# Attention with the probabilities as the stationary operand: sums turned by DMA, projected in three fp16 passes, auxiliary units spread in six slots

## The reference, cut to what matters

```python
q = layernorm(x) @ w_q;  k = ctx @ w_k;  v = ctx @ w_v           # 16 heads of 64
attn = softmax(q k^T / 8)                                        # over 1444 context rows
x = x + tanh(g_xattn) * ((attn v) @ w_o + b_o)
X = layernorm(x)
X2 = X + self_attention(rmsnorm(X, norm1_w)) @ wo                # 16 heads of 8, over 100 tokens
h2 = rmsnorm(X2, norm2_w)
moe = shared(h2) + top-2 of 8 experts(h2)                        # each silu(h2 wg) * (h2 wu) @ wd
out = x + tanh(g_ffn) * (X2 + moe)
```

## Time and profile before

| | us |
|---|---|
| median of 3 runs (1532.3 to 1535.36) | 1532.89 |
| the profiled execution | 1536.03 |
| its span on the core, first to last instruction | 1534.3 |
| a batch in the middle | 79.2, or 81.2 with the loop's turn |
| TensorE, DVE, ScalarE, POOL busy in the span | 1374, 1060, 810, 580 |

### The profile page before, as it was taken

One profiled execution on the slowest core, in us unless ns is written; L12 is line 12 of the kernel. 1 busy time (PEld: TensorE's weight loads), 2 busy tenths in 40 slices (PEclk: granted clock), 3 DMA queues, 4 the chain that ended last, 5 costly groups with the idle time before them and its releaser, 6 DMA issues.

```text
span 1534.3 us, 28786 instructions
## 1 busy us (share of the span) xinstructions
PE 1374.3 (90%) x8776; PEld 839.2 (55%) x8776; DVE 1060.1 (69%) x1996; ACT 810.3 (53%) x1188; POOL 580.3 (38%) x702
## 2 busy tenths in 40 slices
PE   4769999999999999999999999899999999888898
PEld 4225555555555565555555555555555555456676
DVE  2777777767676767676767777677767676866665
ACT  1134646555555555555555565556565655554554
POOL 3023334333433434343334333434333433453454
PEclk7579999999999999999999999999999999899999
DMA  7020202020202010010202020202020100000000
GB/s 216 24 56 1 56 1 57 1 58 1 57 1 58 1 32 25 19 39 2 56 2 57 1 57 1 57 1 57 1 58 1 42 1 1 1 1 1 7 7 11
DMA packets 66966, 43.26 MB, mean 28 GB/s; under 512 B 52966, under 2 KB 62410, under 8 KB 66826
## 3 DMA queue, kind: packets, MB, share of 16 engines
q1 hardware_dynamic: 66826, 41.43, 10.7%
HBM read 15.38 MB, written 0.82 MB: 11 GB/s over the span
## 4 chain that ended last, share of the span: by engine, by line
PE 58%; DVE 18%; issue 12%; ACT 4%; POOL 3%; DMA 2%; DVEq 1%; SPq 0%; ACTq 0%; POOLq 0%
PE psum L756 15%; DVE mx L1240 7%; PE psum L816 7%; PE psum L737 6%; PE psum L741 6%; PE psum L739 6%; PE psum L769 4%; PE psum L856 3%; PE psum L808 3%; PE psum L782 3%; PE psum L843 3%; ACT p_hi L952 2%; DVE y_sb L1262 2%; POOL y_sum L575 2%; DVE mx L1274 1%
## 5 line engine op out<-in xcount | busy, mean ns | idle before, releaser
L951 ACT ACTIVATE p<-psum 128x800 f32<-128x800 f32 x384 | 321.1, 836 | 557.2 <-PE psum L741 555.2
L1240 DVE TENSOR_REDUCE mx<-psum 128x1 f32<-128x512 f32 (+1 forms) x624 | 387.6, 654 | 59.2 <-PE psum L816 55.3
L432 POOL TENSOR_TENSOR p_lo<-p,p_hi 128x800 f16<-128x800 f32 x128 | 244.0, 1906 | 482.3 <-ACT p_hi L952 469.3
L756 PE MATMUL psum<-p_hi,c_both 128*128 128x400 f16 x1536 | 390.3, 336 | 26.3 <-POOL p_lo L432 18.0
L952 ACT ACTIVATE p_hi<-psum 128x800 f16<-128x800 f32 x384 | 319.4, 832 | 0.0
L432 DVE TENSOR_TENSOR p_lo<-p,p_hi 128x800 f16<-128x800 f32 x256 | 258.8, 1011 | 54.6 <-issue 20.1
L816 PE MATMUL psum<-cT_both,qk_hi 96*128 96x512 f16 (+1 forms) x624 | 233.2, 388 | 67.3 <-DVE y_sb L1262 19.5
L756 PEld LDWEIGHTS psum<-p_hi,c_both 128*128 128x128 f16 x1536 | 146.7, 98 | 146.0 <-POOL p_lo L432 24.3
L737 PE MATMUL psum<-qk_hi,cT_both 97*128 97x400 f16 x768 | 195.2, 335 | 14.0 <-issue 9.5
L756 PE MATMUL psum<-p_lo,c_both 128*128 128x400 f16 x768 | 194.9, 335 | 0.0
L739 PE MATMUL psum<-qk_lo,cT_both 96*128 96x400 f16 x768 | 194.5, 334 | 0.0
(11 more groups left out here) (183 smaller groups left out, 1774.9 us busy)
## 6 DMA issues: line engine op xcount, KB each, us to landing
c_both<-c_new SPq DMA_DIRECT2D x16, 768.0 KB, 4.0
ctx_nat<-in_ctx_dram SPq DMA_DIRECT2D x16, 528.0 KB
wg<-in_L_ffn_e_gate_dram SPq DMA_DIRECT2D x1, 1024.0 KB, 5.3
wu<-in_L_ffn_e_up_dram SPq DMA_DIRECT2D x1, 1024.0 KB, 7.3
wd<-in_L_ffn_e_down_dram SPq DMA_DIRECT2D x8, 128.0 KB, 4.9
out_dram<-x SPq DMA_DIRECT2D x4, 200.0 KB
x<-in_x_dram SPq DMA_DIRECT2D x1, 600.0 KB
p<-in_L_xattn_w_q_dram SPq DMA_DIRECT2D x1, 512.0 KB, 3.8
```

What stands on the lines that cost most here:

```text
L432: engine.tensor_tensor(p_lo[0:m, i % 3, :, :], p32[0:m, i % 3, :, :], p_hi[0:m, i % 3, :, :], ALU.subtract).then_inc(lo_made(b, i)[0], 1)
L756: t = mm(outs[k], w[parity][0:m, j, :], p[0:m, i % 3, k, :], start=(j == 0 and w is c_hi and p is p_hi), stop=(j == CH - 1 and w is c_lo))
L951: a(p32[0:m, i % 3, :, :], src, ACT.Exp, scale=DH ** -0.5)
L1240: v.tensor_reduce(mx[:, rt, part:part + 1], bank[:, 0:w], AX.X, ALU.max)\
```

## The change

The product is turned round. Tiles of 128 (head, token) rows of the probabilities become the stationary operand and the context chunk, 97 columns wide (96 for its low part), moves. The 1600 rows make 6 tiles in the first half and 7 in the second (the last one padded), so the scores take 384 and 416 columns per matmul. The passes are p_hi c_hi, p_hi c_lo, p_lo c_hi, and p_lo is waited for only ahead of the third. The sums then lie with (head, token) on partitions. ScalarE copies them in two instructions, POOL's `normalise` multiplies them by the reciprocals and splits them in hi and lo, and SP turns both by DMA (`turn`) into aT. The projection is one auxiliary unit per half (7 and 9 heads), three fp16 passes per head summed in PSUM, and one DVE instruction adds it to x. add_heads, the reciprocals and the products with them are gone.

Auxiliary units are cut in sixths: after the first and second score pass, after the scores, after the first and second product pass, and at the end. y1 stands in unit 7, y0 in 20, ln in 8, and f one unit later up to unit 20. POOL makes the low part of nine units; norm_1 stands ahead of unit 9's, behind those of 5 and 7.

```diff
-    YB = [(0, 1, 2), (3, 4, 5), (6, 7)]
-    YW = D + 1
+    TILES, PER_BANK = (6, 7), (3, 4)
+    WIDE = (6 * P // 2, (ROWS - 6 * P) // 2)
+    ROW0 = (0, 6 * P)
+    PW = 2 * WIDE[1]
+    Y_HEADS = (range(0, 7), range(7, H))
+    Y_SCALE = 256.0
...
-    for n, i in enumerate((2, 3, 4)):
-        plan[i].append(("y1", n))
-    for n, i in enumerate((15, 16, 17)):
-        plan[i].append(("y0", n))
-    plan[6].append(("ln", 0))
-    plan[8].append(("xf", 0))
-    for n, i in enumerate((8, 9, 10, 11, 12, 13, 12, 13, 14, 15, 14, 15, 16, 17, 18, 19, 23)):
+    plan[7].append(("y1", 0))
+    plan[20].append(("y0", 0))
+    plan[8].append(("ln", 0))
+    plan[9].append(("xf", 0))
+    for n, i in enumerate((9, 10, 11, 12, 13, 14, 13, 14, 15, 16, 15, 16, 17, 18, 19, 20, 23)):
         plan[i].append(("f", n))
-    plan[20].append(("rs", 0))
+    plan[21].append(("rs", 0))
     plan[22].append(("h2", 0))
...
-    CTX_AT, Y0_AT = 0, 18
-    LO_POOL = (6, 8, 10, 12, 14, 16, 18, 20)
+    CTX_AT, NORM1_AT, ACC0_AT, NORM2_AT = 0, 8, 14, 22
+    LO_POOL = (5, 7, 9, 11, 13, 16, 18, 20, 22)
...
+    for n, unit in enumerate([("y1", 0), ("ln", 0), ("xf", 0)] + [("f", n) for n in range(16)] +
...
-        thirds = [[us[len(us) * k // 3:len(us) * (k + 1) // 3] for k in range(3)] for us in by_place]
-        return thirds, at
+        sixths = [[us[-(-len(us) * k // 6):-(-len(us) * (k + 1) // 6)] for k in range(6)] for us in by_place]
+        return sixths, at
...
         qk_hi = [sb(f"qk_hi{q}", [C + 1, RT * P], F16) for q in range(2)]
         qk_lo = [sb(f"qk_lo{q}", [C, ROWS], F16) for q in range(2)]
-        p32 = sb("p32", [P, 3, 2, GW])
-        p_hi = sb("p_hi", [P, 3, 2, GW], F16)
-        p_lo = sb("p_lo", [P, 3, 2, GW], F16)
-        acc_sb = [sb(f"acc_sb{g}", [C + 1, 2, GW]) for g in range(2)]
+        p32 = sb("p32", [P, 3, PW])
+        p_hi = sb("p_hi", [P, 3, TILES[1] * P], F16)
+        p_lo = sb("p_lo", [P, 3, TILES[1] * P], F16)
+        acc_sb = sb("acc_sb", [P, TILES[1], C + 1])
+        acc_rc = sb("acc_rc", [P, TILES[1]])
+        minus_one = sb("minus_one", [P, TILES[1]])
+        a_new = sb("a_new", [P, 2, TILES[1], P], F16)
+        aT = sb("aT", [P, 2, sum(TILES) * P], F16)
         mx = sb("mx", [P, RT, MP])
...
+            def turn(b, half):
+
+                t0, t1 = ROW0[half], ROW0[half] + TILES[half] * P
+                for k in range(2):
+                    wait_apart(sp, acc_norm, (b * 2 + half) * 2 + (k + 1))
+                    sp.dma_start_transpose(aT[:, k, t0:t1].rearrange("p (j k) -> p j k", k=P),
+                                           a_new[:, k, 0:TILES[half], :].rearrange("p j c -> p (j c)")).then_inc(at_in, 16)
...
                 for b, kind, parity in ((r * 2 + 1, "odd", 1), (r * 2 + 2, "even", 0)):
                     ctx_made(b + 1, 1 - parity)
+                    turn(b - 1, 1)
+                    turn(b, 0)
                     row_of(b, kind, parity)
...
+            def normalise(b, half):
+
+                n, at = TILES[half], b * 2 + half
+                sums, rc = acc_sb[:, 0:n, 0:C], acc_rc[:, 0:n].unsqueeze(2).broadcast_to([P, n, C])
+                hi, lo = (a_new[:, k, 0:n, 0:C] for k in range(2))
+                pool.wait_ge(acc_out, at + 1)
+                g.tensor_tensor(acc_rc[:, 0:n], acc_sb[:, 0:n, C], minus_one[:, 0:n], ALU.pow).then_inc(acc_rcp, 1)
+                if not (isinstance(b, int) and b == 0 and half == 0):
+                    pool.wait_ge(at_in, at * 32)
+                wait_apart(pool, acc_rcp, at * 2 + 1)
+                g.tensor_tensor(hi, sums, rc, ALU.mult).then_inc(acc_norm, 1)
+                g.tensor_tensor(sums, sums, rc, ALU.mult).then_inc(acc_rcp, 1)
+                pool.wait_ge(acc_norm, at * 2 + 1)
+                wait_apart(pool, acc_rcp, at * 2 + 2)
+                g.tensor_tensor(lo, sums, hi, ALU.subtract).then_inc(acc_norm, 1)
...
                 if kind != "first":
-                    for n in range(len(YB)):
-                        add_heads(b - 1, 1, n, free_of)
-                    norm_1(b - 1)
+                    normalise(b - 1, 1)
                 for i in range(UNITS):
-                    if i == Y0_AT:
-                        if kind == "first":
-                            set_wait(pool, set_dve, SET_DVE, "x1 3")
-                        for n in range(len(YB)):
-                            add_heads(b, 0, n, free_of)
+                    if i == NORM1_AT and kind != "first":
+                        norm_1(b - 1)
+                    if i == ACC0_AT:
+                        normalise(b, 0)
+                    if i == NORM2_AT and kind != "first":
+                        norm_2(b - 1)
                     if i == 9 and kind == "last":
                         inputs_lo(0)
                     if i in LO_POOL:
                         probs_rest(pool, g, b, i)
...
-                    norm_2(b - 1)
...
+            normalise(B - 1, 1)
...
+                between(0)
...
+                between(1)
...
+                half = i // CH
+                for k3, (p, c, wide) in enumerate(((p_hi, c_hi, C + 1), (p_hi, c_lo, C), (p_lo, c_hi, C + 1))):
+                    if p is p_lo:
+                        pe.wait_ge(*lo_made(b, i))
+                    for n in range(TILES[half]):
+                        bank, k = divmod(n, PER_BANK[half])
+                        t = mm(psum[:, ACCB + bank, k * (C + 1):k * (C + 1) + wide],
+                               p[0:m, i % 3, n * P:(n + 1) * P], c[parity][0:m, j, 0:wide],
+                               start=(j == 0 and k == 0 and c is c_hi and p is p_hi),
+                               stop=(j == CH - 1 and p is p_lo), skip_group_check=True)
+                    if k3 < 2:
+                        between(3 + k3)
...
+                    heads = Y_HEADS[half]
+                    pe.wait_ge(at_in, (b * 2 + (half + 1)) * 32)
+                    for h in heads:
+                        hi, lo = (aT[0:C, k, h * S:(h + 1) * S] for k in range(2))
+                        for a, w in ((hi, Nh_hi), (hi, Nh_lo), (lo, Nh_hi)):
+                            t = mm(bank[0:S, 0:D], a, w[:, h, :], start=(h == heads[0] and a is hi and w is Nh_hi),
+                                   stop=(h == heads[-1] and a is lo))
...
+                    slots = steps(kind)[0][i]
+
+                    def between(n):
+                        run_aux(aux, slots[n], b, kind, parity)
+
+                    score_unit(b, parity, i, between)
+                    between(2)
                     if i >= 2:
...
-                a(acc_sb[half][:, :, :], psum[0:C + 1, ACCB:ACCB + 2, 0:GW], ACT.Copy).then_inc(acc_out, 1)
+                if not (isinstance(b, int) and b == 0 and half == 0):
+                    act.wait_ge(acc_norm, (b * 2 + half) * 2)
+                for bank in range(2):
+                    t0, t1 = bank * PER_BANK[half], min(TILES[half], (bank + 1) * PER_BANK[half])
+                    ins = a(acc_sb[:, t0:t1, :], psum[:, ACCB + bank, 0:(t1 - t0) * (C + 1)].rearrange(
+                        "p (k c) -> p k c", c=C + 1), ACT.Copy)
+                ins.then_inc(acc_out, 1)
...
+                    for slot in steps(kind)[0][i]:
+                        run_aux(aux, slot, b, kind, parity)
...
-                    wait_apart(dve, y_add, (b + 1) * 2 * HALF)
+                    wait_apart(dve, aux_free, out_of(("y1", 0)))
...
-
-                    half = int(kind[1])
-                    nh = len(YB[n])
-                    heads = bank[0:S, 0:nh * YW].rearrange("p (k w) -> p k w", w=YW)
-                    at = half * len(YB) + n
+                    xb = x1[:, bat(b), :].squeeze(1)
                     dve.wait_ge(aux_free, free)
-                    v.reciprocal(y_rc[:, 0:nh], heads[:, :, D]).then_inc(y_rcp, 1)
-                    if not (isinstance(b, int) and b == 0 and at < 2):
-                        dve.wait_ge(y_add, b * 2 * HALF + (Y_READ[at - 2] - 2 * HALF * (at < 2)))
-                    dve.wait_ge(y_rcp, b * 2 * len(YB) + (at + 1))
-                    tt(y_sb[:, at % 2, 0:nh, :], heads[:, :, 0:D],
-                       y_rc[:, 0:nh].unsqueeze(2).broadcast_to([S, nh, D]), ALU.mult).then_inc(aux_free, 1)
+                    stt(xb, bank[0:S, 0:D], 1 / Y_SCALE, xb, ALU.mult, ALU.add).then_inc(aux_free, 1)
...
+                    slots = steps(kind)[0][i]
+                    for slot in slots[0:4]:
+                        run_aux(aux, slot, b, kind, parity)
                     if i and i - 1 not in LO_POOL:
                         probs_rest(dve, v, b, i - 1)
                     elif not i and kind != "first":
                         probs_rest(dve, v, b - 1, UNITS - 1)
...
-                    run_aux(aux, three, b, kind, parity)
+                    for slot in slots[4:]:
+                        run_aux(aux, slot, b, kind, parity)
```

## The result

The changed kernel takes 1725.2 us (median of 4 runs, 1722.0 to 1735.3) where the kernel before takes 1534.1 (4 runs, 1532.3 to 1538.0): ratio 1.125, 95% interval 1.120 to 1.131. It is 191 us slower, and far above the forecast's 1565 and its range of 1487 to 1620. The profiled execution took 1724.9 us, its span 1723.2.

The account below looks back on a forecast made before the run. TensorE, 90% busy, bounds the kernel. Per batch 5.2 us fewer columns against holes of 14.4 for 8.0: +17 in 14 batches; ends -3 and +6, clock +12, from 1536.0 to 1568, median 1565 us; range 1487 to 1620.

Parts of the forecast that it names:

- Columns: TensorE's matmul work: 97-column matmuls at 43 ns and a cheaper projection save 5.2 us per batch, leaving 66.0.
- rival C: Small matmuls don't run at column rate: 1625 us at 56 ns each, near 1800 at 80 ns; chance 0.08.
- Item 1: ScalarE serves auxiliary copies only after its exponentials, so TensorE waits in units 13 to 16: 6.7 us per batch.
- Item 2: q units standing inside the scores of units 0 and 1 wait behind ScalarE's exponentials: 1.6 us per batch.
- Item 3: TensorE's transposition of hn waits for norm_1, on POOL behind unit 7's low part: 4.0 us per batch.
- Item 4: TensorE waits for y1, behind reciprocals, products and SP's DMA transposition: 0.3 us per batch, between 0 and 2.
- Item 5: kbd, 1.8 us on DVE behind a shorter unit, and its echo two units on: 1.1 us per batch.
- the rest: TensorE's waits for mneg and for maxima: 0.7 us per batch, where the kernel before had 1.5.
- The sum of the new holes: All TensorE holes of a batch in the new order: 14.4 us where 8.0 were.
- The holes of the kernel before: TensorE's holes in an old batch: 8.0 us, what 71.2 us of counted work leaves of 79.2.
- Ends: Outside the repeated batches: first batch -3 us, last batch even, tail behind the last product +6 us.
- Clock: TensorE dips to half clock behind a hole once in every second batch, 1.7 us each: +12 us, between 0 and +24.

Follow-up runs that it names:

- e2_filler: Changed kernel plus 28, 32 and 28 matmuls with unread results ahead of three waits for the copy to pT in units 14 to 16: 1660.6 us.
- e3_before_sixths: Kernel before, old product and projection, with the auxiliary units in the changed kernel's six slots and its DVE order: 1710.0 us, ratio 1.115.
- e1_thirds: Changed kernel with the auxiliary units back in three places per unit instead of six slots: 1571.2 us, ratio 1.025.
- e6_dve_order: e1_thirds with DVE's order of the kernel before, the low part between the first and second group of auxiliary units: 1554.3 us.

## Why the prediction was wrong, point by point

- **Columns: the rate right, the saving a little too large.** 43 ns for a matmul of 97 columns; rival C was wrong. A batch saves 4.3 us for 5.2, 13 in 14 batches; where the 0.9 is was not looked for. The Trainium skill's 81 ns per matmul ("TensorE: Matmul & The Clock Gate", Back-to-back issue gap) is for 128 columns; this stream of 97 runs at about half of that, and for 128 the 56 ns of the earlier trace rows stand against it.
- **Item 1, ScalarE's units: right.** Forecast 1.9 us three times and 1.0; measured 1.67, 1.93, 1.66 and 0.96, 6.2 a batch for 6.7.
- **Item 2, q: near.** 1.6 forecast; in two batches 0.8 for qk_lo, 1.2 for the accumulator copies and 0.4 for a low part, 1.2 a batch.
- **Item 3, norm_1: the mechanism right, the size too large.** 2.2 us for 4.0. From POOL's low part to TensorE's transposition it is 5.6 us (282.07 to 287.68) where I had 6.6 for the same steps.
- **Item 4, y1: right,** no wait in a batch. But a power of 7 took 3.88 us where I had at most 1.9, in a stretch in which DVE computes low parts too (POOL's timeline, start and length):

```profile
265.59 3.88 POOL L597 TENSOR_TENSOR acc_rc<-acc_sb,minus_one 128x7 f32<-128x7 f32 x1 [4.67 <-ACT acc_sb L980]
```

- **Item 5 and the rest: kbd 0.6 for 1.1, the rest too small.** mneg took 1.2 us a batch and the maxima 2.1, for 0.7 in all. With the turn of the loop, 2.9 us where it was 1.9, this makes up for items 2 and 3.
- **The sum of the new holes: right, in part by luck.** 14.4 x 2 + 2 = 30.8 us for two batches, measured 30.0; but hn is 1.8 a batch too high in it, and the maxima with mneg are 2.6 too low.
- **The holes of the kernel before: wrong, 45 us.** "The remaining 8.0 us are holes of 0.1 to 1.1 us" was what 71.2 us of counted columns left of 79.2. The waits in the old timeline add up to 10.8 us in two batches, 1.9 of them at the turn, so 4.5 a batch; the other 3.5 were TensorE's own work that my count of columns lacked (74.8 us, not 71.2). The new list was walked hole by hole and the old one was a remainder, and their difference, 6.4 a batch, was too small: measured it is 9.6. That is 3.2 x 14 = 45 us.
- **Ends: two errors.** The start lost 5 us instead of gaining 3, which no run went into. "The last one: even" was wrong: hn waits for 7.4 us there, xf taking 2.58 us beside POOL's subtraction of 1200 elements (rows below). y1 waits 9.7 us, and the tail grew by 4.4 for 6.
- **Clock: the step that failed.** "I take one such dip in every second batch, 1.7 us each: +12; between 0 and +24." By two batches it is 16.6 us, 116 in 14 batches. I had taken the price from the one dip that the old trace shows, 3.5 us behind one wait of 2.16, and looked for its like among single holes, of which only hn's seemed long enough. I did not ask what three holes of 1 to 1.9 us within 10 us do, and a fourth behind them, though my own list had them in a row in units 13 to 16. The clock drops behind them for 13.7 us or more in every batch, and e2_filler shows that it is the idle time. The old trace had nothing like it, so the term's bound was an extrapolation from one case, and the range had no room for it.

With 116 us for the clock in place of 12, the old holes at their sum, and the columns as measured, the forecast's own sum is 1565 + 104 + 45 + 13 = 1727 us, for 1725 measured. The three terms come from the same two batches and add up by construction; that the clock's follows the idle time is what e2_filler shows.

## What to carry to other kernels

A piece of work that an in-order engine serves only behind its long instructions must stand behind the work those wait for; spreading such pieces evenly over TensorE's list leaves the list full and the engine idle. Take both lists of holes, of before and after, by the same method. Price several holes in a row together, as a stretch at half clock, and not each by its own length: here the clock cost nearly as much as the holes. When moving a short urgent step forward on POOL, look at what POOL then runs beside the DVE steps that follow it.

## What the runs showed of the hardware

- Idle time of TensorE in pieces of 1 to 1.9 us, three within some 10 us, was followed by 13.7 us at 1.2 GHz; in every second batch 6.8 us at 1.2 GHz came already behind the second of them. Filled with matmuls whose result nobody reads, most of these stretches ran at 2.4 GHz, and the kernel was 65 us faster with 67 us more work.
- DVE's `hn`, 0.34 us alone, took 1.72 beside POOL's low part, and `xf`, 0.35, took 2.58 beside a POOL subtraction of 1200 elements (the last batch of the changed kernel):

```profile
1501.01 2.58 DVE L1207 TENSOR_SCALAR xf<-x,aggr,ps 100x128 f32<-100x128 f32 x1 [2.22 <-POOL ps L624]
1501.05 2.45 POOL L647 TENSOR_TENSOR cT_both<-h2T,c_both 128x1200 f16<-128x1200 f32 x1
```
- The loop's turn became longer, with 1599 matmuls in two batches for 921: 1.6 to 2.2 us of idle time before, 2.8 to 3.2 after. In e3_before_sixths, with the old product, it stayed at 1.8 to 2.0, so the slots don't do it. In e1_thirds there is another wait without a releaser behind it (timeline, TensorE):

```profile
655.70 0.50 PE L749 MATMUL psum<-qk_hi,cT_both 97*128 97x384 f16 x2 [2.86 <-issue]
...
658.59 0.99 PE L826 MATMUL psum<-xlnT,Mh 128*96 x5 [1.03 <-issue]
```

Whether the number of instructions does it was not tried and stays open. Open as well is why DVE follows the row maxima worse than in the kernel before: 20 to 53 us of waits in all versions with the turned product, 9.4 before and 10.5 with the slots on the old product. DVE's order makes 17 of it (e6_dve_order). For the rest a shorter unit on TensorE with the same maxima per batch fits, and so does the other set of units on POOL, which no run separated.
